# One exponential instruction for four heads, an earlier maximum of logits and later bias copies in a fused conv-attention, attention and MoE kernel

## The reference, cut to what matters

```python
# layer 0: attention with 8 heads of 16 channels over the 768 tokens of a batch
att = einsum('bhqd,bhkd->bhqk', q, k) / sqrt(hd) + bias_t + bias_p   # causal in time
y = softmax(att) @ v
x = x + (y @ Wo)                                        # inputs: group norm of x
# layer 1: additive attention, 16 hidden units
hidden = tanh(A[:, :, None, :] + B[:, None, :, :])       # 768 x 768 x 16 a batch
logits = einsum('bijh,h->bij', hidden, w2) + b2
t = t + softmax(logits) @ v                             # inputs: layer norm of t
# layer 2: mixture of experts, 8 experts, the best 2 a token, gelu, capacity 1920
t = t + moe(layernorm(t))
```

## Time and profile before

| | |
|---|---|
| median of 3 runs | 2275.16 us (2265.41 to 2275.72) |
| the profiled execution | 2264.8 us, span 2263.0 us |
| busy in the span: PE | 2056.6 us (91%) |
| DVE | 1550.5 us (69%) |
| ACT | 1682.2 us (74%) |
| POOL | 1535.5 us (68%) |
| TensorE clock granted, mean | 0.979 of full speed |
| exponentials of scores (L945) | 768, 391.5 us |
| exponentials of logits (L952) | 96, 86.8 us, 84.0 us idle before them |
| maximum and ring reductions (L1324) | 704, 451.0 us |

### The profile page before, as it was taken

How to read it: one execution, slowest core, us unless ns; L and a number is a source line. 1 busy time by engine, 2 the same in 40 slices (tenths; PEclk the granted TensorE clock), 3 DMA queues, 4 the chain that set the end, 5 groups by cost and what they waited for, 6 DMA issues and landing times.

```text
span 2263.0 us, 54452 instructions
## 1 busy us (share of the span) xinstructions
PE 2056.6 (91%) x19545; PEld 1203.6 (53%) x19545; DVE 1550.5 (69%) x4167; ACT 1682.2 (74%) x1966; POOL 1535.5 (68%) x1907
## 2 busy tenths in 40 slices
PE   4889999999999999999999999999999978799996
PEld 2555555555555555455555555555545443367775
DVE  7786777777777787878787878787867554324343
ACT  4449888888887878888888888888879998524332
POOL 5117667677676767676767676767677876347777
PEclk8799999999999999999999999999999999999998
DMA  4746322222322232223223232323221000035553
GB/s 108 111 86 145 93 46 69 48 63 47 72 50 72 51 71 51 71 52 69 53 63 59 61 60 60 58 59 54 58 44 26 13 5 6 24 57 87 85 88 34
DMA packets 157429, 137.41 MB, mean 61 GB/s; under 512 B 24666, under 2 KB 149815, under 8 KB 157105
## 3 DMA queue, kind: packets, MB, share of 16 engines
q1 hardware_dynamic: 119376, 109.87, 23.8%
q0 software_dynamic: 23824, 16.85, 5.4%
q10 hardware_dynamic: 13968, 7.30, 1.3%
HBM read 82.68 MB, written 54.52 MB: 61 GB/s over the span
## 4 chain that ended last, share of the span: by engine, by line
PE 29%; DVE 18%; issue 16%; POOL 14%; POOLq 10%; DVEq 5%; ACT 5%; DMA 1%; another core or an unknown queue 0%; SPq 0%; ACTq 0%
POOL hidden L847 10%; PE logits L1052 8%; POOLq L846 7%; POOL out_dram L601 4%; DVE max_halves L1324 3%; PE av_bank L1038 3%; PE ring L1130 3%; PE ring L1144 2%; ACT hidden L969 2%; PE scores L1022 2%; PE scores L1025 2%; ACT hidden L976 2%; PE ring L1152 2%; PE ring L1121 1%; DVE logit_bias L1510 1%
## 5 line engine op out<-in xcount | busy, mean ns | idle before, releaser
L847 POOL TENSOR_SCALAR hidden<-b_rep,a_cols 128x768 f32<-128x768 f32 x1120 | 1026.8, 921 | 415.3 <-issue 232.2
L969 ACT ACTIVATE hidden<-hidden 128x2304 f32<-128x2304 f32 (+1 forms) x384 | 796.1, 2073 | 52.9 <-POOL hidden L847 52.8
L1052 PE MATMUL logits<-hidden,w_shifted 128*32 128x384 f32 x6144 | 580.6, 494 | 58.2 <-ACT hidden L976 31.1
L1324 DVE TENSOR_REDUCE max_halves<-ring 128x4 f32<-128x512 f32 (+1 forms) x704 | 451.0, 659 | 156.8 <-PE ring L1130 150.9
L945 ACT ACTIVATE probs<-scores 128x512 f32<-128x512 f32 (+1 forms) x768 | 391.5, 547 | 202.5 <-PE scores L1025 195.9
L976 ACT ACTIVATE hidden<-b_rep,a_cols 128x768 f32<-128x768 f32 x416 | 385.0, 933 | 0.0
L1052 PEld LDWEIGHTS logits<-hidden,w_shifted 128*32 128x32 f32 x6144 | 163.4, 109 | 290.8 <-issue 227.4
L1130 PE MATMUL ring<-k_max,q_max 112*128 112x128 bf16 x2688 | 270.3, 223 | 17.2 <-DVE max_halves L1324 12.8
L1022 PE MATMUL scores<-bias_q,onehot_k 112*128 112x512 bf16 (+1 forms) x768 | 273.9, 357 | 4.1 <-DMA q_parts<-max_parts 1.8
L1025 PE MATMUL scores<-q_parts,k_parts 98*128 98x256 bf16 (+1 forms) x1536 | 275.0, 260 | 0.0
L1130 PEld LDWEIGHTS ring<-k_max,q_max 112*128 112x128 bf16 x2688 | 180.9, 99 | 157.9 <-issue 66.3
(11 more groups left out here) (274 smaller groups left out, 2611.7 us busy)
## 6 DMA issues: line engine op xcount, KB each, us to landing
qk_parts<-qk_parts_sb SPq DMA_DIRECT2D x16, 1152.0 KB, 4.3
q_parts<-qk_parts SPq DMA_DIRECT2D x192, 96.0 KB, 3.2
k_parts<-qk_parts SPq DMA_DIRECT2D x192, 96.0 KB, 4.4
q_max<-qk_parts SPq DMA_DIRECT2D x96, 96.0 KB
k_max<-qk_parts SPq DMA_DIRECT2D x96, 96.0 KB
expert_rows<-clear_row ACTq DMA_DIRECT2D x9, 792.0 KB, 5.2
x_in<-in_x_dram SPq DMA_DIRECT2D x96, 64.0 KB
x<-in_x_dram SPq DMA_DIRECT2D x96, 64.0 KB
```

What stands on the lines that cost most here:

```text
L847: last = g.tensor_scalar(hidden[:, q % SLOTS, o, :], b_rep[:, side], 1.0, a_cols[:, side, a_col(q, o):a_col(q, o) + 1], ALU.mult, ALU.add)
L969: s.activation(hidden[:, t % SLOTS, 0:n_, :], hidden[:, t % SLOTS, 0:n_, :], ACT.Tanh)
L1052: last = mm(logits[32 * g:32 * g + 32, half, 0:HALF], w2_shifted[:, k, :], hidden[:, q % SLOTS, g, HALF * half:HALF * half + HALF], start= ...
L1324: v.tensor_reduce(max_halves[:, h % 4:h % 4 + n_, BLOCK_PAIRS.index((qb, kb))], bank[:, 0:n_ * P].rearrange("p (h k) -> p h k", h=n_), AX. ...
```

## The change

`exp_scores` is called once a tick. It waits until both banks are filled, then takes one exponential over two banks and four heads (1024 columns, or 512 where the step has 128 queries) and raises `scores_read` by 2. DVE's maximum of logits is moved ahead of the ring reads of slot 0 (before, it stood behind those of slot 1). POOL waits for `parts_ready` of 4 before the eight bias copies.

```diff
--- before.py
+++ after.py
@@ -825,6 +825,7 @@
                 g.tensor_tensor(tn_all, tn_hi, tn_mid, ALU.add)
                 pool.drain()
                 g.memset(flag[:, 0:1], 0.0).then_inc(bias_made, 1)
+                pool.wait_ge(parts_ready, 4)
                 for h in range(H):
                     last = g.tensor_copy(bias_q[0:64, h, :].rearrange("p (b n t) -> p b n t", n=16, t=8),
                                          tn_all[0:64, :].rearrange("p (w h) -> p w h", h=H)[:, :, h][:, ::-1]
@@ -935,16 +936,15 @@
                     act.wait_ge(made, 5)
                 act.dma_start(cleared[k], clear_source).then_inc(rows_cleared, 16)
 
-            def exp_scores(c, d, pair):
+            def exp_scores(c, d):
                 n_ = STEPS[d][4]
-                act.wait_ge(scores_filled, c * 48 + (2 * d + pair + 1))
-                if pair == 0:
-
-                    if positive(count := c * 24 + (d - 2)):
-                        act.wait_ge(av_done, count)
-                s.activation(probs0[:, d % 3, 2 * pair:2 * pair + 2, 0:n_],
-                             scores[:, pair].rearrange("p (j l) -> p j l", j=2)[:, :, 0:n_], ACT.Exp) \
-                 .then_inc(scores_read, 1)
+                act.wait_ge(scores_filled, c * 48 + (2 * d + 2))
+
+                if positive(count := c * 24 + (d - 2)):
+                    act.wait_ge(av_done, count)
+                s.activation(probs0[:, d % 3, :, 0:n_],
+                             scores[:].rearrange("p a (j l) -> p (a j) l", j=2)[:, :, 0:n_], ACT.Exp) \
+                 .then_inc(scores_read, 2)
 
             def exp_logits(b, blk):
 
@@ -956,8 +956,7 @@
                 for t in ps.ticks:
                     stage, d = score_step(t, EXP_AT)
                     if ps.has(stage):
-                        exp_scores(ps.batch(stage), d, 0)
-                        exp_scores(ps.batch(stage), d, 1)
+                        exp_scores(ps.batch(stage), d)
                     if ps.has("end") and t == 1:
                         exp_logits(ps.batch("end"), 5)
                     if ps.has("add") and ps.has("mid") and t >= 5 and t % 4 == 1:
@@ -1499,10 +1498,7 @@
                     x1_ = x1[:, ps.side("mid")]
                     half = slice(0, 3) if t < 15 else slice(3, 6)
                     for slot in range(PARTS):
-                        for use in parts[slot]:
-                            if ps.has(use[0]):
-                                read(ps, use)
-                        if t % 4 == 0 and slot == 1 and ps.has(stage) and blk >= 0:
+                        if t % 4 == 0 and slot == 0 and ps.has(stage) and blk >= 0:
                             c = ps.batch(stage)
                             dve.wait_ge(logits_added, c * 24 + 4 * (blk + 1))
                             if positive(count := c * 6 + blk):
@@ -1511,6 +1507,9 @@
                             dve.drain()
                             v.tensor_scalar(logit_bias[:, 1:2], logit_bias[:, 0:1], b2_col[:], b2_col[:], ALU.subtract,
                                             ALU.add).then_inc(max1_ready, 1)
+                        for use in parts[slot]:
+                            if ps.has(use[0]):
+                                read(ps, use)
                         if (ps.has("mid") or ps.has("add")) and t == 4 and slot == 3:
                             norm_seed(1)
                         elif not ps.has("mid") and not ps.has("add") and (t, slot) in NORM_AT:
```

## The result

| | before | after |
|---|---|---|
| median (runs) | 2272.25 us (4: 2265.41 to 2275.72) | 2298.99 us (4: 2292.14 to 2304.21) |
| ratio | | 1.013 [1.0097, 1.0163] |
| profiled execution, span | 2264.8, 2263.0 us | 2299.95, 2298.2 us |
| first addition of logits starts | 171.5 us | 180.7 us |
| mean of a full pass | 115.8 us | 117.9 us |

The changed kernel is slower by 1.3%, 27 us on the medians. The spans of the two profiled executions lie 35.2 us apart, and the traces say where: the head is 9.2 us longer (to the first addition of logits), the twelve full passes 26.2 (2.19 each), the last two passes 4.8; the first pass with logits is 2.2 us shorter and the end 2.8.

What follows compares the result with a forecast made beforehand. PE (TensorE) was taken to bound the kernel. The terms 5.0 + 2.3 + 3.5 + 0.8 - 2.5 - 0.7 - 1.1 = +7.3 us, on a median of 2275.16, gave 2282.5 us, range 2260 to 2297.

Steps and rivals of the forecast that it cites:

- the maximum ahead of the ring reads: DVE's maximum of logits in each pass: moved forward, it delays ring readers 0 to 1.3 us a time; taken as 0.
- The give-back at tick 8: Tick 8 of full passes: 0.94 us returns as PE's longer wait for tanh(7); net -2.5 us, bounds -13.2 and 0.
- the early gain: Ticks 0 to 5 of each pass: earlier exp_logits and no ring-bank wait at tick 1 save 0.94 us a pass.
- The head: 74 to 190 us: PE refills bank 0 late; +5.0 us until 98 us (0 to 5.0), then +2.3 (0 to 4.5).
- The merge in the passes: One exponential of 1024 columns takes 1.03 us, 0.92 until the next; tick 17 costs +3.5 us over 14 passes.
- Tick 17's wait: Tick 17 of each pass: PE waits about 0.4 us for ACT's exponentials before the scores' first matmul.
- The bias copies: Near 53 us: POOL's copies wait, so DVE's second subtraction shortens from about 1.68 to 0.6; -1.1 us, bounds -1.7 and 0.
- The slower one: Head and tick 17: the wait for bank 1 passes through; 18.7 us, 2294 us, up to 2302; chance 0.28.
- the refill at tick 17: Tick 17 of each pass, in the slower rival: PE's late refill of bank 0 costs 9.2 us; chance 0.28.
- the ring fills of tick 12: Tick 12, in the slower rival: ring fills also wait for the moved maximum, up to 0.6 us a pass (+8).
- ACT sets the pace: Full passes: ACT bounds them, so gains at ticks 0 to 5 stay; 10 to 14 us faster, 2262 us; chance 0.22.
- the 0.6 us that I had named as a sign of being wrong: Full passes: growth of over 0.6 us each would show the forecast wrong.

Runs made afterwards that it cites:

- 16 alone: The kernel before with only the maximum of tick 16 moved ahead of the ring reads; ratio 1.0092.
- 0 and 4 moved: The kernel before with only the maxima of ticks 0 and 4 moved ahead of the ring reads; ratio 1.0050.
- three repairs: The whole change, but exponentials merged only in passes with logits to add, tick 16's maximum at its old place, x1 loads after tick 5's logits; 2277.60 us, ratio 1.0035.

## Why the prediction was wrong

Forecast: 2282.5 us, 2260 to 2297; measured 2298.99, outside. Its sum was +7.3 us, measured +27 to +35.

- **The failed step** is in "the maximum ahead of the ring reads": "I take 0: at ticks 12 and 20 DVE is behind already and the sum of its work is the same". I had named the split piece of tick 16 as queued behind the wait and then not priced it, because the argument was made only for ring reads. The sum of DVE's work is the same, but the order isn't neutral: the piece used to fill the time until the logits were there. Behind the wait it makes DVE 0.73 us late, and being late it meets POOL: the normalised heads take 1.85 to 2.33 us instead of 0.86. Together that costs 1.99 us a pass (16 alone), 24 us over twelve passes, where my upper bound, 1.3 us a time, gives 16.
- **The give-back at tick 8** was right in its kind: the early gain was 0.78 us (forecast 0.94) and came back there. Its bound on the slow side, 0, was wrong. The argument "tanh(7) doesn't move with ticks 0 to 5" looked at POOL's own events, and the earlier trace rows, and not at what TensorE's earlier progress moves against them: ticks 7 and 8 took 1.6 us with 0 and 4 moved. The net cost is 0.88 us a pass with 0 and 4 alone moved, in the whole change less: 1.21 lost and 0.78 won.
- **The head** came to +9.2 us, forecast +7.3 (5.0 and 2.3), bounds 0 to 9.5. The number is near by luck. With only the merge, the waits are 1.9 us up to 98 us, in five waits of 0.25 to 0.75 us, where I had ten gaps and 5.0; behind it they are 5.5 where I had 4.5, and other waits take up part of them, as I had assumed. The net is 4.2 us of idle time. The clock, 2.7 us in the changed kernel and 3.7 with only the merge, had no term: I had priced every gap at one duration and left the clock as it was.
- **The merge in the passes**: the durations are nearly exact (1.02 us, forecast 1.03; 0.91 to the next, forecast 0.92). Tick 17's wait was forecast as 0.4 us, measured

```profile
1069.33 0.39 PE L1021 MATMUL scores<-bias_q,onehot_k 112*128 112x512 bf16 x1 [0.27 <-ACT probs L945]
...
1073.05 1.50 PE L1051 MATMUL logits<-hidden,w_shifted 128*32 128x384 f32 x16 [0.24 <-ACT hidden L975]
...
1076.54 0.64 PE L1037 MATMUL av_bank<-probs,v_aug 128*32 128x256 f32 x8 [0.46 <-DVE headsT_raw L1495]
```

  (the third is tick 18's wait of the failed step). The +0.4 us of tick 17 (forecast 0.25) is where it was put, but with the merge in the passes alone ticks 18 and 21 take it back: +3.5 forecast, about 0 measured.
- **The bias copies** (forecast -1.1): the pair of subtractions shortened by 1.45 us (2.86 to 1.41), and the maxima behind it start 2.1 us earlier, but the last copies, 2 us later, meet two small steps that took 0.17 us each:

```profile
50.79 1.41 DVE L1410 TENSOR_TENSOR qk_parts_sb<-x_in,qk_parts_sb 128x384 bf16<-128x384 f32 x2
...
63.13 1.26 DVE L1258 TENSOR_SCALAR ln_small<-ln_mv 128x6 f32<-128x6 f32 x1
64.46 1.34 DVE L1260 TENSOR_SCALAR ln_small<-ln_small 128x7 int32<-128x7 int32 x1
```

  The first scores start at 75.43 us, before at 75.28. By itself the part measures 0.9999. In this trace the wait isn't even what held the copies: the subtractions are through at 52.2 us, and POOL's last step ahead of the copies ends at 54.2. Over all kernels here POOL gets there between 51.3 and 54.3 us, whatever the change. Where it comes early and nothing holds it, the copies fall on the last cast and on both subtractions: these take 1.84 and 3.45 us in the run with the maximum only, against 1.21 and 1.19 in the one with three repairs, which waits. The first scores then start at 77.8 to 78.2 instead of 74.9 to 75.9. Five of the twelve traces without the wait show that, none of the six with it. So the wait is worth some 2.5 us where POOL comes early, and that is part of the scatter of the first addition; the medians don't show it.
- **The rivals.** The slower one, 2294 us at 0.28, came nearest in time, but by another mechanism: of its places only the head bears a loss as priced (9.5, measured 9.2); the refill at tick 17 and the ring fills of tick 12 don't (moving 12 costs nothing). "ACT sets the pace" is refuted: once the head, tick 16 and the send are out of the way, the merge gains nothing. The passes grew by 2.19 us each, over the 0.6 us that I had named as a sign of being wrong.

## What to carry to other kernels

When a wait is moved forward in an engine's queue, list everything behind it and ask of each piece what it was doing at its old place: independent work that stood ahead of the wait was filling it, and behind the wait it comes on top. Price that piece by itself even if the engine's sum of work is unchanged. And a small gain on one engine shifts everything that is tied to its progress, loads and instruction fetches too, against engines that don't move; before counting a lost gain as "comes back, no more", look for what will now coincide.

## What the runs showed of the hardware

- One packet of the queue listed as "instruction" (16384 bytes, 0.9 to 1.7 us) that starts among a send's 32 packets can hold one to three of these until it ends (69 of 77 passes), and a drain behind the send waits for them, 1.0 to 2.0 us. Where 31 or more packets have started before it, none is held (91 passes).
- A POOL drain behind such a send waited some 2 and 4 us in every pass where the DMA engines were full (share 1.01), 0.25 us where they weren't.
- PE's granted clock in the head went from 0.50 to 1.00 at about 79.3 us without waits, and at about 84.8 and 86.8 us in the two kernels where PE had stopped for 0.75 or 0.76 and for 0.32 us on the way: two stops of 1.1 us together cost 2.7 and 3.7 us more through the clock.
- DVE's steps on 6 or 7 columns, 0.17 us alone, took 0.56 to 1.34 us beside POOL's copies or sums, and three of 128x128 took 1.85 us and more instead of 0.86, so for such steps what runs on POOL decides, not their size.
